# Output-projection matmuls of an attention stage: issued from the fifth key block of a head instead of the second

## The reference, cut to what matters

```python
xn = _layernorm(x)
s = _L0_attn_ref(xn, Wq, Wk, Wv, Wo)      # 16 query heads, 4 key/value heads, rotary, no mask
g = _silu(_L0_ffn_ref(xn, ...))           # 16 experts, top 4, plus shared experts
x = x + s * g
xn = _layernorm(x)
s = _L1_attn_ref(xn, W_qkv, b_qkv, W_out, b_out)   # 16 heads, causal mask
g = _silu(_L1_ffn_ref(xn, ...))           # int8-range weights, gate/up/down
x = x + s * g
# attention: softmax(Q K^T / 8) V, all heads joined, times the output weights
```

## Time and profile before

| | us |
|---|---|
| median of 2 runs | 4871.51 (4870.26 and 4872.77) |
| the profiled execution, its own time | 4884.0 |
| its slowest core (core 3), first to last instruction | 4882.4 |
| the other seven cores | 4843.5 to 4862.2 |
| layer 0: heads of chunks 0 to 3 | from about 2245 to 3195 |
| layer 1: heads of chunks 0 to 3 | from about 4115 to 4832 |
| PE, ACT, DVE busy, share of the span | 75%, 27%, 26% |

### The profile page before, as it was taken

The page is one execution under the profiler, slowest core; times in us unless marked ns, Lnnn a source line. Parts: engine busy times, 40 slices in busy tenths (PEclk is TensorE's granted clock), DMA queues, the critical chain, the costliest instruction groups (busy, mean ns, idle before and its releaser), DMA issues.

```text
span 4882.4 us, 44353 instructions; the slowest of 8 cores (4843.5 to 4882.4 us)
## 1 busy us (share of the span) xinstructions
PE 3666.5 (75%) x14712; PEld 1453.8 (30%) x14712; DVE 1286.5 (26%) x2076; ACT 1328.9 (27%) x1573; POOL 281.1 (6%) x522
## 2 busy tenths in 40 slices
PE   2246667899999999976777777742999966667775
PEld 0012223344444444432222222211444422222221
DVE  3333320033033023112222222225101023443323
ACT  1100000011011011004666666611111101455663
POOL 1000000000000000000000000000101000000000
PEclk9878888999999999988988888865999999788998
DMA  3257778744434434430011111134444420122212
GB/s 76 63 148 198 210 197 198 177 144 147 155 121 145 148 135 142 138 108 9 15 29 35 35 35 35 31 88 110 74 82 66 80 47 9 26 52 44 44 37 63
DMA packets 139086, 450.92 MB, mean 92 GB/s; under 512 B 15568, under 2 KB 15728, under 8 KB 122480
## 3 DMA queue, kind: packets, MB, share of 16 engines
q0 software_dynamic: 73632, 218.42, 21.7%
q1 hardware_dynamic: 65232, 229.67, 13.6%
HBM read 490.23 MB, written 73.40 MB: 115 GB/s over the span
## 4 chain that ended last, share of the span: by engine, by line
PE 54%; DMA 15%; DVE 14%; ACT 10%; issue 5%; DVEq 1%; SPq 0%; ACTq 0%; POOL 0%; POOLq 0%
ACT a16t L1524 8%; PE pst L747 8%; PE pst L761 8%; PE pst L863 4%; PE pb L863 4%; DMA a32t<-l_u 4%; PE pb L1004 3%; PE pst L940 3%; PE pb L1467 3%; PE pst L951 3%; PE pst L1493 3%; PE pst L1498 3%; DMA a16t<-s_g 2%; PE pb L1249 2%; PE pst L1381 2%
## 5 line engine op out<-in xcount | busy, mean ns | idle before, releaser
L1524 ACT ACTIVATE a16t<-pst 128x1024 bf16<-128x1024 f32 x832 | 852.1, 1024 | 563.9 <-PE pst L1498 497.5
L747 PE MATMUL pst<-xn_sb,a16t 128*128 128x512 bf16 x2304 | 595.3, 405 | 192.5 <-DVE a16t L695 162.4
L761 PE MATMUL pst<-xn_sb,a16t 128*128 128x512 bf16 x2304 | 558.7, 386 | 0.0
L1467 PE MATMUL pb<-a16t 128*65 128x512 bf16 x832 | 346.0, 416 | 176.7 <-DVE a16t L1541 96.2
L1493 PE MATMUL pst<-a16t 128*128 128x512 bf16 x832 | 351.6, 423 | 163.2 <-DVE a16t L1426 103.4
L774 ACT ACTIVATE a32t<-pst 128x512 f32<-128x512 f32 x288 | 172.0, 597 | 1108.3 <-PE pst L747 1108.3
L782 DVE TENSOR_TENSOR a32t<-a32t,pst 128x512 f32<-128x512 f32 x256 | 176.0, 688 | 1115.9 <-PE pst L761 1110.0
L747 PEld LDWEIGHTS pst<-xn_sb,a16t 128*128 128x128 bf16 x2304 | 227.0, 102 | 508.5 <-issue 287.1
L1498 PE MATMUL pst<-a16t 128*128 128x512 bf16 x832 | 353.7, 425 | 0.0
L1472 PE MATMUL pb<-a16t 128*65 128x512 bf16 x832 | 341.1, 410 | 0.0
L761 PEld LDWEIGHTS pst<-xn_sb,a16t 128*128 128x128 bf16 x2304 | 230.6, 100 | 290.8 <-issue 33.5
(11 more groups left out here) (156 smaller groups left out, 2803.8 us busy)
## 6 DMA issues: line engine op xcount, KB each, us to landing
a16t<-s_g POOLq DMA_DIRECT2D x108, 512.0 KB, 5.0
a16t<-s_u SPq DMA_DIRECT2D x108, 512.0 KB, 3.2
a32t<-l_u SPq DMA_DIRECT2D x32, 1024.0 KB, 10.0
a16t<-s_d SPq DMA_DIRECT2D x27, 1024.0 KB, 4.9
a16t<-s_d POOLq DMA_DIRECT2D x27, 1024.0 KB, 5.2
s_g<-a16t SPq DMA_DIRECT2D x36, 512.0 KB, 7.7
s_u<-a16t SPq DMA_DIRECT2D x36, 512.0 KB, 8.4
s_d<-a16t SPq DMA_DIRECT2D x18, 1024.0 KB, 8.0
```

Of the source, the lines that this page charges most:

```text
L747: li = t.matmul(pb[gp_][:, :], a16t[:, o_gb[wp] + hc * 256 + ici * 128: o_gb[wp] + hc * 256 + ici * 128 + 128], xn_sb[:, hc * T + tc * TC: ...
L761: li = t.matmul(pb[up_][:, :], a16t[:, o_ub[wp] + hc * 256 + ici * 128: o_ub[wp] + hc * 256 + ici * 128 + 128], xn_sb[:, hc * T + tc * TC: ...
L1467: t.matmul(av_a[0:65, :], a16t[:, o_vtm + kc * 65 * nvh + kva * 65: o_vtm + kc * 65 * nvh + kva * 65 + 65], a16t[:, o_pt[kp4]:o_pt[kp4] + TC],
L1524: return s.activation(a16t[:, o_pt[kp4]:o_pt[kp4] + 2 * TC], pst[kp][:, 0:1024], AF.Exp, scale=0.125)
```

## The change

One place in the `kc` loop. Before, each `kc` from 1 on adds `av(kc-1)` and then one projection unit. Now `av(kc-1)` stays where it is, no unit is added at `kc` 1 to 3, one at each `kc` from 4 on, and a second one at the last two blocks of the head.

```diff
                         if kc >= 1:
                             emit_av(kc - 1)
+                        if kc >= 4:
                             emit_unit()
+                            if kc >= nkc - 2:
+                                emit_unit()
```

## The result

The changed kernel takes 0.979 of the time of the kernel before, with a 95% interval of 0.976 to 0.982: 4871.5 x 0.979 = 4770 us where 4754 was forecast, 102 us less instead of 118. (Some executions of either kernel are several per cent longer on one die or both, at a lower granted clock; ratios leave those out, and where only one die was at it, the cores of the other are read.) The profiled execution took 4774.9 us beside 4884.0, its slowest core 4773.3 beside 4882.4.

What follows compares the result with a forecast made beforehand. In the attention stages TensorE delivers late, partly at the lower clock, and ACT waits. Savings of 54 (layer 0) + 16 + 22 + 26 (layer 1 chunks 3, 2, 1) = 118 us take 4871.5 to about 4754, range 4730 to 4796.

Steps and rivals of the forecast that it cites:

- The wait as the cause: All 48 heads with units lose the first unit's wait for DVE's second multiply (L1615), 51.0 us in all before.
- Layer 0, 28.4 us: Layer 0's 24 heads with units go from 30.66 to 28.4 us each, saving 54 us (bounds 28 and 64).
- Heads at the upper clock in layer 1: Without the 1.67 us wait, such heads take 17.2, 21.7 and 26.4 us in chunks 1, 2 and 3.
- the lower clock in layer 1: Added to upper-clock head lengths: 0.3 us in chunk 1, 0.4 in chunks 2 and 3, with one idle stretch fewer.
- Doubled units, later finishes and loads: Second units in layer 1 chunks 1 and 2 cost 5 us; later DVE finishes, stores and POOL weight loads cost nothing.
- Rival A: Only the wait goes, clock as now: layer 0 saves 26 us, layer 1 31, about 4814 us; chance 0.20.
- Rival C: Heads too thin at their start stay at 1.2 GHz, 11.5 us a head; all layer 0 about 5083 us; chance 0.02.
- D: No change, the wait turning up elsewhere (kc 4 weights, doubled units): within 20 us of 4871; chance 0.03.
- Rival B: Layer 0 heads all 28.0 us, layer 1 always at upper clock: saves 136, 4735 us; counted in the forecast's 0.75.

Runs made afterwards that it cites:

- wait2: Changed kernel with the third score matmul pair again waiting for DVE's multiplies, units left in place: layer 0 heads 30.34 us, cores 4 to 7 4836 to 4857 us.
- single: Changed kernel without the second unit in the last two blocks of a head: 4766 to 4773 us, 0.978 of the kernel before.
- fill_after: Changed kernel with thrown-away matmuls (10 in layer 0, 5 in layer 1) ahead of each head's first score matmul: 0.969 of the kernel before.

## Why the prediction was right, and where a size was off

- *The wait as the cause.* Right: `wait2` brings back 2.06 of 2.38 us a layer 0 head with nothing but the wait.
- *Layer 0, 28.4 us.* Measured 28.28, between the bounds of 28.0 and 29.5. The forecast let two heads in three be near 28.0 and one at 29.1, for which it gave no row. The trace has 17 of 24 at 27.6 to 28.4 us, with a mean clock of 0.94, and seven at 28.7 to 29.1, with 0.88; two in a row:

```profile
2492.00:2519.60 27.60, 21.36 (x83) 7.43 (x84) 7.57 (x11) 18.62 (x19) 1.06 (x2) 0.94 0.19 38
2519.60:2548.70 29.10, 22.79 (x83) 7.99 (x83) 7.57 (x11) 18.62 (x19) 1.06 (x2) 0.88 0.18 37
```

- *Heads at the upper clock in layer 1.* 26.4 was measured as 26.33, 21.7 as 21.91, 17.2 as 17.43. The 1.67 us of the wait were taken from one head of chunk 3 and held there; in chunk 2 the same difference is 0.2 less (23.16 - 21.91 + 0.2 = 1.45). Chunk 1's length was put together from chunk 2's, with no head of its own to read, and is 0.2 short.
- *The term that was mis-sized* is the lower clock in layer 1, the "0.4 for the lower clock, which now has one idle stretch fewer to fall in" of chunks 2 and 3 and the 0.3 of chunk 1. Measured against the heads at the upper clock it is 22.71 - 21.91 = 0.8, 27.01 - 26.33 = 0.7 and 17.96 - 17.43 = 0.5; on most other cores chunk 3 is at 27.36, 1.0 above, as much as the lower clock cost there before (28.83 - 27.85). The step that failed is the reason given, "one idle stretch fewer to fall in". In the kernel before, the hole in an upper-clock head begins 2.6 us after the first score matmul (3.90 less 1.30), yet in three of the four heads of chunk 3 that lost the clock it had fallen before that. One of them, timeline and windows:

```profile
4655.11 0.38 PE L1493 MATMUL pst<-a16t 128*128 128x512 bf16 x1 [1.83 <-DVE a16t L1440]
...
4656.69 0.59 PE L1594 MATMUL pb<-a16t,cst 128*128 128x512 bf16 x1 [0.55 <-DVE a16t L1569]
...
4656.80:4663.50 6.70, 5.82 (x14) 1.94 (x13) 1.37 (x2) 2.48 (x4) 0.00 (x0) 0.50 0.11 21
```

  Taking the hole away could not save these falls. In the changed kernel the clock still falls in four heads of chunk 3 on this core, and in six on most others; but it is up again after about half the time, and such a head is 27.6 or 27.7 us, 1.3 or 1.4 above one at the upper clock, where three of the four took 29.9 or more, at least 2.1 above. In chunks 1 and 2 the falls did become fewer: by core, 6 to 9 in chunk 1 and 6 or 7 in chunk 2 before, 2 or 3 and 2 or 4 after. One head of chunk 3, ahead of the fall, where PE is busy for 3.79 of 7.60 us, and in its low part:

```profile
4606.00:4613.60 7.60, 3.79 (x16) 1.48 (x18) 5.58 (x9) 3.83 (x5) 0.53 (x1) 1.00 0.35 84
...
4613.80:4617.00 3.20, 3.20 (x9) 1.29 (x8) 1.37 (x2) 1.82 (x2) 0.00 (x0) 0.50 0.18 33
```

  Why the clock falls in some of these heads and not in others is open: no run here shows it.

  This term is 8 x (0.2 + 0.4 + 0.3) = 7 us, and the 0.2 short on the heads of chunks 1 and 2 are 3 more: layer 1's 54 us instead of 64. Layer 0 gave 3 more than forecast.
- *Doubled units, later finishes and loads.* The doubled units were priced at 5 us and the others at nothing; `single` shows the first to be as small as that, and in the changed kernel L1249 waits for weights 2 times, 5.4 us, where it was 2 and 6.3.
- *Rival A* (only the wait goes, the clock does as before) falls by the granted clock of 0.92 and by heads of 28.28 where it gave 29.5, but it had more in it than its chance said: with the clock held up the wait alone makes up nearly two thirds of layer 0's gain, and 67 us in all where A gave 57. *Rival C* (too thin to rise) falls by the same rows, *D* by the result. *Rival B*'s step, the clock always up, is what `fill_after` then built: heads of 27.10 in layer 0, below even B's 28.0, because B kept the low stretch at the head's start.

## What to carry to other kernels

When work is woven into a loop to fill an engine's gaps, the first piece must stand where its inputs are ready in time: everything behind it in that engine's queue shares its wait, and here that was the pair of score matmuls that feeds the engine which sets the pace. One block later is enough; further back brings nothing. A wait of 0.9 us on TensorE, early in a head, cost 2.4 us here: 1.5 as the delay of what stands behind it, 0.9 as a granted clock that came back later. Where TensorE must wait for another engine anyhow, matmuls that compute nothing can hold the clock up; here they cost no time.

## What was not expected of the hardware

Ten and five matmuls of 512 columns that fill 2.1 of 3.2 us and 1.1 of 1.8 us of idle held the granted clock at 1.00 in the changed kernel over nearly all heads with units, and in the kernel before over 19 of 24 in layer 0. No time was lost to them: layer 0's heads without units went from 27.24 to 26.37 us, and the whole program, on all eight cores at once, to 0.969.
